# Moving the small v_pv copies and the presplit subtraction off GpSimd in an eight-core attention and MoE block

## The reference

```python
xn = _layernorm(x)                       # no scale, no bias
x  = x + attn(xn) + ffn(xn)

# attn: 16 heads of 64; the softmax runs over the HEADS of one token, not over tokens
q, k, v = split(xn @ w_qkv.T)            # each b, n, 16, 64
a = softmax(einsum('bnhd,bngd->bnhg', q, k) * 64**-0.5)
o = einsum('bnhg,bngd->bnhd', a, v)
o = swapaxes(o, 1, 2).reshape(b, n, d)   # heads ahead of tokens
return o @ w_proj.T + b_proj

# ffn: 8 experts of 512, top 2 of them with sigmoid scores and 2 groups,
#      and a shared expert of 2048; squared ReLU
routed = einsum('tei,ehi,te->th', relu(x @ up)**2, down, cw)
shared = relu(x @ shared_up.T)**2 @ shared_down.T
```

## Time and profile before

| what | us |
|---|---|
| timed, median of 2 runs | 4717.0 |
| timed, lowest and highest | 4710.56 and 4723.45 |
| the profiled execution, its own time | 4264.87 |
| its span on the slowest core (core 7) | 4263.3 |
| spans of the 8 cores | 4205.7 to 4263.3 |

### The profile page before, as it was taken

How to read it: one execution, slowest core, us unless ns; L and a number is a source line. 1 busy time by engine, 2 the same in 40 slices (tenths; PEclk the granted TensorE clock), 3 DMA queues, 4 the chain that set the end, 5 groups by cost and what they waited for, 6 DMA issues and landing times.

```text
span 4263.3 us, 47284 instructions; the slowest of 8 cores (4205.7 to 4263.3 us)
## 1 busy us (share of the span) xinstructions
PE 3366.3 (79%) x16592; PEld 1836.8 (43%) x16592; DVE 910.0 (21%) x2094; ACT 581.9 (14%) x1190; POOL 360.4 (8%) x372
## 2 busy tenths in 40 slices
PE   4577757576656666659999969999879999899997
PEld 2354535353535454434444434444434444344443
DVE  2121111111111111042222241222322222312222
ACT  1120111121212020211100110011111111110010
POOL 1000031312222222200000000000000000000000
PEclk8668776868686868669999979999899999899998
DMA  5325263636364545522222222323322222322322
GB/s 151 124 80 157 66 216 109 200 126 217 119 197 139 187 159 175 181 80 99 80 89 96 92 99 96 102 94 104 114 74 91 97 80 89 109 79 95 110 87 94
DMA packets 172627, 506.88 MB, mean 119 GB/s; under 512 B 36056, under 2 KB 52568, under 8 KB 172384
## 3 DMA queue, kind: packets, MB, share of 16 engines
q1 hardware_dynamic: 121840, 415.69, 29.7%
q0 software_dynamic: 24832, 79.77, 5.1%
q10 hardware_dynamic: 25728, 8.39, 1.7%
HBM read 411.44 MB, written 75.50 MB: 114 GB/s over the span
## 4 chain that ended last, share of the span: by engine, by line
PE 66%; DMA 14%; DVE 5%; issue 5%; ACT 4%; ACTq 2%; POOL 2%; SPq 0%; DVEq 0%; POOLq 0%
PE p L286 57%; DMA wb<-sqk 3%; PE p L573 3%; PE p L555 3%; ACTq L462 2%; DMA ARB<-sv 2%; POOL ARB L264 2%; DMA sup_s<-ARB 2%; DMA wbig<-sproj 2%; DMA sdn_s<-ARB 1%; PE p L331 1%; PE p L888 1%; ACT AR L566 1%; ACT ARB L260 1%; DMA ssup<-ARB 1%
## 5 line engine op out<-in xcount | busy, mean ns | idle before, releaser
L286 PE MATMUL p<-ARB,wb 128*128 128x512 bf16 (+1 forms) x7680 | 1523.5, 366 | 475.9 <-DMA wb<-sqk 230.2
L286 PEld LDWEIGHTS p<-ARB,wb 128*128 128x128 bf16 x7680 | 813.1, 107 | 1200.0 <-issue 602.3
L286 PE MATMUL p<-ARB,wbig 128*128 128x512 bf16 (+1 forms) x6144 | 1217.5, 361 | 87.7 <-DMA wbig<-sproj 27.1
L286 PEld LDWEIGHTS p<-ARB,wbig 128*128 128x128 bf16 x6144 | 613.1, 101 | 689.4 <-issue 125.2
L914 ACT ACTIVATE AR<-AR 128x512 f32<-128x512 f32 x128 | 80.8, 631 | 1202.8 <-DVE AR L909 1202.8
L264 POOL TENSOR_TENSOR ARB<-AR,ARB 128x1024 bf16<-128x1024 f32 x96 | 203.2, 2116 | 312.0 <-ACT ARB L260 311.7
L286 PE MATMUL p<-ARB 128*128 128x512 bf16 x768 | 184.8, 397 | 54.4 <-DMA ARB<-sv 38.1
L999 POOL DMA_DIRECT2D out<-AR x16 | 8.5, 531 | 2473.0 <-DVE AR L986 2473.0
L950 DVE TENSOR_TENSOR AR<-p,AR 128x512 f32<-128x512 f32 x128 | 88.5, 692 | 529.1 <-PE p L286 510.0
L573 PE MATMUL p<-AR 128*128 128x65 f32 x512 | 124.3, 422 | 78.5 <-ACT AR L566 78.5
L909 DVE TENSOR_SCALAR AR<-p 128x512 f32<-128x512 f32 x128 | 88.5, 692 | 353.6 <-PE p L286 353.6
(11 more groups left out here) (89 smaller groups left out, 1203.7 us busy)
## 6 DMA issues: line engine op xcount, KB each, us to landing
wb<-sup_s SPq DMA_DIRECT2D x128, 512.0 KB, 4.4
wbig<-sdn_s SPq DMA_DIRECT2D x128, 512.0 KB, 3.7
wb<-sqk SPq DMA_DIRECT2D x112, 512.0 KB, 7.6
wb<-ssup SPq DMA_DIRECT2D x64, 512.0 KB, 4.2
wbig<-ssdn SPq DMA_DIRECT2D x64, 512.0 KB, 3.8
ARB<-sv SPq DMA_DIRECT2D x56, 512.0 KB, 4.1
wbig<-sproj SPq DMA_DIRECT2D x56, 512.0 KB, 3.7
AR<-wup SPq DMA_DIRECT2D x32, 512.0 KB, 6.0
```

The lines of the kernel that those rows point to most:

```text
L286: E.matmul(psum_ap, wa, xa_, start=(first_flag and i == 0), stop=(stop_flag and i == 2)),
```

## The change

In `presplit` the subtraction moves from GpSimd to VectorE, with its wait for the cast. GpSimd's wait for the subtraction, ahead of the write that it issues, stays. In the `v_pv` copies GpSimd's 16 issues for each block move to ScalarE, which then issues all 32; the two semaphores stay apart, and GpSimd's wait ahead of them goes away. No byte that is moved and no value that is computed changes.

```diff
@@ presplit
-            W("gpsimd", thi)
-            tlo = bd.do("gpsimd", lambda E, fs=fs, ps=ps:
+            W("vector", thi)
+            tlo = bd.do("vector", lambda E, fs=fs, ps=ps:
                         E.tensor_sub(spl[:, 2048 * ps + 1024:2048 * ps + 2048],
                                      wsf[:, 1024 * fs:1024 * fs + 1024],
                                      spl[:, 2048 * ps:2048 * ps + 1024]), "P", 1)
@@ v_pv copies, in each attention block
             t_vev = tv
-            W("gpsimd", t_vev, v_ones, last["v_pv"])
             W("scalar", t_vev, v_ones, last["v_pv"])
             t_vpv = {}
             for g in range(16):
                 for tsub in range(2):
-                    eng, sem = (("gpsimd", "PV") if (2 * g + tsub) % 2 == 0
+                    eng, sem = (("scalar", "PV") if (2 * g + tsub) % 2 == 0
                                 else ("scalar", "PV2"))
                     t_vpv[sem] = bd.do(eng, lambda E, g=g, tsub=tsub:
                                        E.dma_start(
```

## The result

The changed kernel takes 4312.9 us in the median of 11 runs (4300.1 to 4616.3). Its time is 1.0086 times that of the kernel before, with a 95% interval of 1.0067 to 1.0105, so it is 29 to 45 us slower, about 37 us. That is within 2% and measurably not zero. The predicted time of 4781 us missed because it starts from 4717 us. Otherwise the kernel before takes 4267 to 4280 us in this comparison, close to its profiled execution of 4264.9 us. The predicted step itself was +64 us.

What follows compares the result with a forecast made beforehand. The prediction took a chain of waits in the attention stage, with ScalarE's issues and the presplit ring on it, as the bound. Issues +89, subtraction -32, block ends +7 give +64 us, so 4717 becomes 4781 us, range 4718 to 4845.

Steps and rivals of the forecast that it cites:

- The base: Whole kernel: the step was added to the timed median of 4717 us, 452 us above the profiled execution of 4264.9.
- The issues: Head of all eight attention blocks: 16 more `v_pv` issues each on ScalarE delay everything behind them, +89 us.
- the 89 us: Forecast cost of the added ScalarE issues over eight blocks, taken between 85 us undisturbed and 93.4 us for the same stretches again.
- My lower bound, 85 us: Added ScalarE issues in eight blocks, each at the 0.667 us of block 7, where the queue runs undisturbed.
- Who waits first: Block starts: bank 0's emptying waits behind the layernorm; in block 7, without layernorm, the first cast waits and the presplit ring starts late.
- The subtraction: Presplit ring, blocks 2 to 7: VectorE does it 0.89 us faster at 36 places on the chain, -32 us.
- The 7 us for the ends of the blocks: VectorE's order at block starts and ends: the subtraction waits about 0.4 us, then delays transposes 0.9 us, in five blocks.
- The ring gains far more than the subtraction: Rival, blocks 2 to 7: second slot's write also goes earlier, 2 us off each turn, about 4717 us; chance 0.13.
- The write gives it back: Rival, presplit ring: the job's write lengthens by what the subtraction gains, +96 us, 4813 us; chance 0.14.
- VectorE's order costs nothing in chunks 0 to 7: Emptying the next chunk's bank behind the subtraction: only chunk 5 late, 0.3 us, counted at nothing; 59 us if wrong.
- ScalarE's queue backing up: Rival, `v_pv` issues: the added ones run at the slow ones' pitch, 137 us, +112 in all, 4829 us; chance 0.13.
- The rule that several issuers save only issue time: Skill's rule for `v_pv` issues: the time saved is usually small; as a rival, added issues hidden, -25 us, 4692 us; chance 0.05.

## Why the prediction was right and wrong

- **The base: wrong, and this is what puts 4312.9 us far outside 4718 to 4845.** The step that failed is the carrying over of the sum to the timed median, 452 us above the profiled execution. What the runs showed in its place: the kernel before takes 4267 to 4280 us, which is the level of the profiled execution, and nothing in its rows had room for the 452. I called it the weakest step, and gave it a place only in the 0.05 for faster. The rows showed a chain of waits and a matmul stage at 0.94 of the clock that add up to 4263 us; an unexplained 10% above a complete account should have had its own case, with the sum made on the profile: 4329 us, 0.4% from what was measured. That it comes so near is in part luck: its step is 64 us, and the measured one 37.
- **The issues: mechanism right, size wrong.** They lie on the path at the head of all eight blocks, and the added time arrives there (stretches +72.2, end of stage +71 us with the issues alone). The mis-sized term is the 89 us, which measured 73.4. I doubled the stretches, and took off only a part of the disturbance for the added half. But GpSimd's copies were what slowed most of ScalarE's own 16, and they are gone too. An undisturbed issue is 20.91 us / 32 = 0.653 us; 256 of them are 167 us, and 167 - 97.6 = 70 would have been nearer. My lower bound, 85 us, was for the same reason not a bound.
- **Who waits first: named only in half.** I said that in block 7 the ring's late start is what counts, and elsewhere bank 0. The version with the layernorm ahead shows that the ring's start holds all six blocks with jobs; bank 0 holds block 1 alone, and in block 0 the casts of the weights stand behind the issues. The price was the same, so the sum didn't suffer. The wait for bank 0, forecast at about 25 us, is 22.4 us.
- **The subtraction: right.** 1.225 us against 1.226 expected; -32 + 7 = -25 us forecast, -18 and -22 us measured. Between first and last write it gives 5 us a block, 28 to 32 in six. The 7 us for the ends of the blocks fit the 1 us a block that the rest gets longer beyond the shift of the last write, though two profiles of one kernel differ by almost as much there. A turn of 11.4 us against 11.9 forecast.
- **The ring gains far more than the subtraction: fell.** It needed 2 us a turn, 16 us a block; the stretch of the ring got 5 us shorter.
- **The write gives it back: fell.** The landing stays at 7.4 us, and the mean of all writes moves from 6.9 to 7.0 us.
- **VectorE's order costs nothing in chunks 0 to 7: right.** On core 6, waits of TensorE for the bank that line 506 empties are 7 in number, as before the change; six are the one at the start of blocks 1 to 6, the seventh is 1.1 us.
- **Blocks with jobs 5 to 6 us longer: right, 5.4.** Blocks without jobs about 11 us longer: block 0 was (+12.1), block 1 not (+4.3), since there before's 16 issues took 15.8 us and after's 32 take 21.3.
- **ScalarE's queue backing up: fell.** The pitch of the added half is the undisturbed one.
- **The rule that several issuers save only issue time: holds, and its "small" doesn't.** The "small" of "DMA: Bandwidth & Descriptors" of the Trainium skill, section "Issuing engines are not separate DMA queues", would have made it -25 us. With the issues alone moved, 72.2 us of issuing cost 71 us, so nothing but issue time was at stake; it was the largest term, because it stood ahead of a ring that was the bound.
- **Stage to metric.** The stage grew by 49 us, the mean span by 43, the timed slowest core by 37 (29 to 45). The slowest of eight cores is not the mean; I made nothing of that in the prediction. The 6 us between the stage and the mean span lie in what follows block 7, where nothing was changed.

## What to carry to other kernels

An issue of a DMA costs ScalarE's queue 0.65 us here and GpSimd's 0.60 us (32 in 19.25 us), although the engine counts as idle: ask what stands behind a row of them, and put it behind the start of whatever ring bounds the stage. Taking the issues off GpSimd, where nobody waited for them, gained no more than the end of some slow issues on ScalarE. What counts is the place: with the subtraction on VectorE, 32 issues in one row on ScalarE make the kernel 0.9% slower than before, and the same 32 there, two behind each chunk, 2% faster. And when the profiled execution and the timed ones differ by 10%, decide first which of them the rows explain.

## What was not expected of the hardware

- Small DMAs issued by GpSimd at the same time made single issues on ScalarE slow: its 16 took 81.8 us in seven blocks beside GpSimd's, 75.3 us without. Block 1 is an exception that was not explained: 15.8 us beside them and 15.9 without, and up to 16.97 us (core 3) without.
- The same copy of 32 KB is cut differently by the two queues. From before to after, q10 grew from 25728 to 43136 packets, 136 for each of 128 copies, while q0 fell from 24832 to 20736, 32 for each; the bytes moved over are 4.2 MB in both. Yet q10's share of the engines' span grew from 1.7% to 2.1%, and q0's fell from 5.1% to 4.3%.
